# Batch 1's token statistics on VectorE: ahead of the first maximum instead of behind the second

## What is computed

```python
x = x + xcond(layernorm(x), ctx, ctx, lens)      # s = SCALE * log(lens)
#   attn = softmax(s * einsum('bhdq,bhdk->bhqk', q, k))
#   out  = einsum('bhqk,bhdk->bhdq', attn, v)
x = x + moe(layernorm(x), Wg, W1, W3, W2, sw1, sw3, sw2)
#   top-1 of 8 experts, 128 rows each, silu(x W1) * (x W3) @ W2, plus a shared expert
```

## Time and profile before

| | |
|---|---|
| median of 3 runs | 159.94 us (159.8 to 160.06) |
| the profiled execution, its own time | 160.61 us |
| its span in the trace | 158.8 us |
| busy: PE, DVE, ACT, POOL | 146.4, 101.9, 86.5, 62.9 us |
| chain that ended last, share by engine | PE 77%, DVE 7%, ACT 5% |
| granted TensorE clock over the span | 0.989 |

### The profile page before, as it was taken

The page is one execution under the profiler, slowest core; times in us unless marked ns, Lnnn a source line. Parts: engine busy times, 40 slices in busy tenths (PEclk is TensorE's granted clock), DMA queues, the critical chain, the costliest instruction groups (busy, mean ns, idle before and its releaser), DMA issues.

```text
span 158.8 us, 3537 instructions
## 1 busy us (share of the span) xinstructions
PE 146.4 (92%) x1291; PEld 102.7 (65%) x1291; DVE 101.9 (64%) x250; ACT 86.5 (55%) x197; POOL 62.9 (40%) x88
## 2 busy tenths in 40 slices
PE   7779999998999999999999998997899999999940
PEld 2445565454555545554555787995799989999820
DVE  0499786689687887875232546677866677776220
ACT  3443265755748575656767198345583386663300
POOL 7115839304607150321010000066598077827550
PEclk9999999999999999999999999999999999999995
DMA  3992534453160700000350878012238712212110
GB/s 81 336 360 70 165 114 132 148 172 107 30 246 11 261 1 5 0 6 0 102 177 2 272 257 287 9 41 93 74 101 221 258 39 84 74 55 91 64 60 33
DMA packets 15824, 18.42 MB, mean 116 GB/s; under 512 B 1980, under 2 KB 15077, under 8 KB 15808
## 3 DMA queue, kind: packets, MB, share of 16 engines
q1 hardware_dynamic: 14368, 14.98, 29.7%
q0 software_dynamic: 1152, 2.97, 5.5%
q10 hardware_dynamic: 288, 0.26, 0.5%
HBM read 14.12 MB, written 4.21 MB: 115 GB/s over the span
## 4 chain that ended last, share of the span: by engine, by line
PE 77%; DVE 7%; ACT 5%; issue 5%; DMA 2%; POOL 1%; SPq 0%; POOLq 0%; DVEq 0%
PE bank L982 17%; PE bank L1019 11%; PE bank L1003 9%; PE bank L1217 5%; PE bank L1157 4%; PE bank L1192 4%; PE bank L1193 4%; PE bank L1071 4%; PE bank L1069 4%; PE bank L934 3%; DMA xs<-in_x 2%; PE bank L1031 2%; PE bank L1046 2%; PE bank L1039 2%; DVE nm L524 2%
## 5 line engine op out<-in xcount | busy, mean ns | idle before, releaser
L524 DVE TENSOR_REDUCE nm<-bank 128x2 f32<-128x512 f32 x64 | 40.9, 685 | 11.2 <-PE bank L982 11.2
L773 ACT ACTIVATE pt<-bank 128x512 f32<-128x512 f32 x64 | 34.5, 589 | 15.8 <-PE bank L1003 15.6
L1003 PE MATMUL bank<-qz,kz 32*128 32x256 f32 x256 | 40.9, 402 | 0.0
L982 PE MATMUL bank<-kz,qz 32*128 32x256 f32 x256 | 35.1, 403 | 0.9 <-DVE qz L502 0.9
L982 PEld LDWEIGHTS bank<-kz,qz 32*128 32x128 f32 x256 | 21.9, 184 | 13.3 <-issue 7.7
L1003 PEld LDWEIGHTS bank<-qz,kz 32*128 32x128 f32 x256 | 24.9, 184 | 4.5 <-ACT pt L773 2.8
L1019 PE MATMUL bank<-pt,vext 128*32 128x256 f32 x256 | 20.2, 391 | 0.0
L437 POOL DMA_INDIRECT expert_rows<-rk,idx_s x8 | 8.0, 1002 | 24.2 <-DVE rk L612 20.6
L373 POOL TENSOR_SCALAR qz<-xs,rs,mrs 128x256 f32<-128x256 f32 x14 | 7.7, 562 | 20.9 <-DVE mrs L496 20.9
L398 POOL TENSOR_SCALAR mrs<-mv,rstd 128x1 f32<-128x1 f32 x6 | 1.6, 260 | 30.5 <-ACT rstd L785 30.5
L464 POOL DMA_INDIRECT vext<-out,rk x8 | 9.7, 1215 | 7.1 <-DMA out<-xs 5.0
(11 more groups left out here) (164 smaller groups left out, 316.9 us busy)
## 6 DMA issues: line engine op xcount, KB each, us to landing
wraw<-in_w SPq DMA_DIRECT2D x10, 352.0 KB, 3.4
wraw<-in_w SPq DMA_DIRECT2D x10, 128.0 KB, 3.4
expert_rows<-zero SPq DMA_DIRECT2D x1, 1032.0 KB, 5.7
out<-xs SPq DMA_DIRECT2D x8, 128.0 KB, 3.1
xs<-in_x SPq DMA_DIRECT2D x3, 256.0 KB, 5.9
cs<-in_ctx SPq DMA_DIRECT2D x3, 256.0 KB, 6.1
wraw<-in_sw SPq DMA_DIRECT2D x2, 352.0 KB, 5.7
kz<-in_w SPq DMA_DIRECT2D x2, 352.0 KB, 4.0
```

What stands on the lines that cost most here:

```text
L524: nc.vector.tensor_reduce(nm[:, b % 2, :, place], scores_bank[:].rearrange("p (u c) -> p u c", u=2), AX_X, ALU.max, negate=True).then_inc( ...
L773: nc.scalar.activation(pt[:, g % NPT, n % 4, :], sc_bank[n % NS][:], ACT.Exp).then_inc(exped, 1)
L982: mm = nc.tensor.matmul(scores_bank[:, u * D:(u + 1) * D], qz[rows, b, half, u * P:(u + 1) * P], kz[rows, b, half, :], start=True, stop=True)
L1003: mm = nc.tensor.matmul(sc_bank[n % NS][:, c * D:(c + 1) * D], kz[rows, b, half, c * P:(c + 1) * P], qz[rows, b, half, :], start=True, sto ...
```

## The change

`query_stats(1)`, the statistics of batch 1, is called once ahead of VectorE's loop, right behind batch 0's queries, in place of inside the loop behind the maxima 0 and 1. The instructions are the same ones with the same waits and signals. No other engine's program is touched. In the changed kernel the lines from L515 to L623 are numbered one higher, and those from L626 on one lower.

```diff
             query_scales(0)
             eager_queries(0)
+            query_stats(1)
 
             def maximum(n):
...
                 if t < TURNS:
                     maximum(2 * t)
                     maximum(2 * t + 1)
-                if t == 0:
-                    query_stats(1)
                 if t == 1:
                     query_scales(1)
                     eager_queries(1)
```

## The result

The changed kernel takes 159.32 us (median), against 159.89 of the kernel before; the ratio of the comparable runs is 0.9946, with a 95% interval of 0.9928 to 0.9965. Measured a second time it took 159.14 against 159.96, ratio 0.9958 (0.9946 to 0.997). One of the six executions behind the 159.32 took 267.93 us; it isn't in the ratio, and without it the median is 159.16. The prediction was 159.1, with a range of 158.8 to 159.6. Its span in the trace is 157.7 us.

A forecast was written before the change was run, and what follows sets the result against it. TensorE sets the attention stage's pace; in the opening it idles 0.93 us for a copy behind late statistics. Of 1.01 us, VectorE's cap leaves 0.85, which off the 159.94 median gives 159.1, range 158.8 to 159.6 us.

The forecast's parts named there:

- The cover: VectorE's 1.28 us wait before the first maximum hides batch 1's statistics, which would cost 0.55 us without it.
- ScalarE: Batch 1's `lnv` starts at 7.33 instead of 9.88; the first `vext` copy runs to about 9.6 instead of 11.88.
- TensorE's transposes: The second transposes (L957), which waited for the `vext` copy, start at 10.91 instead of 11.92, 1.01 us earlier.
- The cap at the maxima's transpose: L991, transposing batch 0's maxima, needs VectorE's eighth maximum: earlier by 0.83 to 0.98 us, 0.85 taken.
- the handover from VectorE to TensorE: Time from VectorE's end to TensorE's start, 0.15 us at the opening (6.73 to 6.88), applied again at L991.
- The first rival: VectorE caps the gain: slower handovers or maxima leave TensorE only VectorE's 0.55 us; 159.4 us, chance 0.14.
- The second check, at 18.56: Scores reusing a bank need the thirteenth maximum: possible from 17.72, TensorE there at 17.73, so nothing more is lost.
- The stages behind: Everything past L991 hangs on TensorE or on what follows L991, so all starts earlier by the same amount.
- The clock: TensorE's granted clock is 1.00 in the first 20 us and from 20 to 88, nothing to gain or lose.
- GpSimd beside the statistics: GpSimd's `qz` L373 (6.63, 0.56 us) now runs beside the statistics; any slowdown from BN_STATS priced at zero.
- the second rival: GpSimd's L373 stands still up to 0.55 us during the statistics; gain down to 0.38, 159.55 us, chance 0.05.
- The slower rival: VectorE waits for x's second chunk; slower from landing at 8.3, 1 us for each us; 160.4 at 8.8, chance 0.05.

The follow-up runs named there:

- e6: Changed kernel with x's second chunk loaded behind the third chunks of x and the context, issued near 3.1 us: 159.08 us, ratio 0.994.
- e1: Kernel before with only ScalarE's order altered, the first values copy ahead of batch 1's rstd and keys: 159.56 us, ratio 0.9974.
- e3: Changed kernel without the four unread matmuls of turn 2 on TensorE: 159.11 us, ratio 0.9946.
- e9: Changed kernel without the four unread matmuls of turn 4: 159.69 us against 160.9 for the kernel before, ratio 0.9917.
- e7: Changed kernel with the first half of batch 1's queries on GpSimd and without turn 2's four unread matmuls: 159.06 us, ratio 0.9934.
- e4: Changed kernel with the load of x's second chunk issued last among the loads of x and the context: 163.39 us, ratio 1.0198.
- e10: Changed kernel with the first half of batch 1's queries on GpSimd, without the unread matmuls of turns 0, 2 and 4: 158.38 us, ratio 0.9904.
- e5: Kernel before with the load of x's second chunk issued last among the loads of x and the context: 162.80 us, ratio 1.0189.
- e8: Changed kernel with the first half of batch 1's queries on GpSimd, without the unread matmuls of turns 0 and 2: 159.78 us against 160.9, ratio 0.991.

## Why the prediction was right, step by step

**The cover.** The statistics were to start at 6.67 and be done near 7.25 ahead of a first maximum at 8.01: 6.65, 7.29 and 8.02. The chunk's landing, bounded at 6.1 to 6.6, was early enough, and e6 shows that 7.5 would have been too.

**ScalarE.** `lnv` at 7.33 as computed, and the copy near 9.6 (9.67).

**TensorE's transposes.** 1.01 us earlier expected, 0.99 measured (11.92, now 10.93).

**The cap at the maxima's transpose.** Range 0.83 to 0.98, taken 0.83 to 0.85, measured 0.89. The mechanism is shown by e1 (with the copy in time, but the maxima as before, 0.38 us are gained at this place, which is the slack between the eighth maximum and L991 in the kernel before) and by e3 (a microsecond less of TensorE's work, no change). VectorE's own 0.51 us (the eighth maximum from 14.01 to 13.50) and that slack of 0.38 make the 0.89. The term that was mis-sized is the handover from VectorE to TensorE: I took the 0.15 us of the opening, and here it is 0.05 (13.50 to 13.55), in e1 0.06. The range had it from 0 to 0.15, and the middle would have been the better choice. The eighth maximum ended at 13.50, not 13.46, which took back 0.04 of these 0.10 us; that 0.85 came so close to 0.89 is in part this. The first rival had the right engine, for VectorE does set this place, but its price of 0.55 left out the slack of 0.38.

**The second check, at 18.56.** It held (17.67, against a bound of 17.72), and e9 shows that the bound is real. But what I concluded from it ahead of e9, that TensorE's queue has nothing more to give there, is wrong by the 0.38 us of e9. It didn't enter the sum.

**The stages behind.** Passed on in full, 0.89 of 0.89 over 83 us.

**The clock.** The prediction read 1.00 for the first 20 us. For the first 5 us that column can't be taken at its word, as the last section shows. Nothing hung on it, since the first scores waited for the queries (0.94 us of idle time ahead of 6.88).

**GpSimd beside the statistics.** L373 took 0.55 us with BN_STATS beside it (6.64, against 0.56 before), so the second rival is out:

```profile
6.64 0.55 POOL L373 TENSOR_SCALAR qz<-xs,rs,mrs 128x256 f32<-128x256 f32 x1 [3.05 <-DVE mrs L496]
```

The one at 10.87 took 0.65 again, beside VectorE's L502; in e7, where L502 is gone, two of them took 1.09 together. That fits the rule of the Trainium skill (GPSIMD Engine Reference, Specifications) that GpSimd contends with VectorE instructions in a 2-port perf mode or with two SBUF inputs, though no row shows in which mode L502 runs. BN_STATS slowed nothing in these traces.

**The slower rival.** Its mechanism is shown by e4, its point at 8.3 us lies between e6 and e4. Its point was worked out with the handover of 0.15; with the 0.05 measured it would be 8.4. Its price of 1 us for each us holds for VectorE's queue (in e4 the eighth maximum ended at 17.06, as computed for T = 11.05), but not for the kernel: the formula gives a loss of 2.75 us (11.05 - 8.3), and it was 3.4, since the clock fell behind TensorE's wait for the banks, which the prediction had left out.

**The time.** The trace's 0.89 us against the 0.85 of the sum is the sharper test. The two ratios put the gain at 0.6 to 1.2 and at 0.5 to 0.9 us, and both medians, 159.32 and 159.14, lie in the range.

## What to carry to other kernels

An operation without a cover can cost its place in the queue twice: once by what waits for its result, once by what stands behind it. Moving it into an idle stretch of its engine gains, at the place where both paths meet, the smaller of what each of them allows there, with the slack that it had counted in: here 0.99 us on TensorE's side, and 0.51 + 0.38 on VectorE's. So compute both and look for that place. When one limit is removed and nothing happens, look for the idle time that opened on the same engine: in e7 the next limit was due within 0.3 us.

## What the runs showed of the hardware

TensorE's granted clock stayed at 1.00 behind an idle time of 0.93 us in the kernel before, of 1.17 in the changed kernel (ahead of its first scores), of 1.54 at the same place in e6, and of 0.45 in e10. It fell to 0.50 in e4, 1.4 us after an idle time of 1.73 us had ended, and in e5 within one of 2.35 us, and the work behind ran at half the speed: 1.91 us for the four unread matmuls instead of 1.03. So a late input costs more than its own delay here. The 1.54 that cost nothing and the 1.73 that did lie close together and behind different work, so these runs don't show at what length an idle time costs the clock.

The clock column says 1.00 from the start of every trace, but the first unread matmuls don't run like it. In the first fence, a view of the kernel before, four of them take 1.91 us, as long as in e5 at 0.50. From near 5 us on they take 1.03 there. The second fence is e6, with the longest idle time that left the clock alone.

```profile
2.69 1.91 PE L934 MATMUL bank<-onesb 128*128 128x512 bf16 x4
```

```profile
7.05 1.58 PE L983 MATMUL bank<-kz,qz 32*128 32x256 f32 x16 [1.54 <-DVE qz L504]
```

None of the unread matmuls of the turns 0, 2 and 4 were needed to keep the clock up here; e8 and e10 ran without a drop in the opening. Whether those of the turns 6 to 9 are was not tried.
